# Second layer of a two-layer graph network: row transposes by DMA, block mask and adjacency joined in SBUF

## The chip, the cores and the metric

The kernel runs on one core of one Trainium2 chip. The metric is the device time of one execution in microseconds (us), as the median of the runs taken. Engines have these names in the rows of the profile: PE is TensorE (matmuls) and PEld its weight load, DVE is VectorE, ACT is ScalarE, POOL is GpSimd, SP is the queue that issues most DMAs. Each engine works through its own list of instructions in order; between engines there are semaphores, on which an instruction waits until a count is reached.

## The reference

N = 2048 nodes with D = 256 features; adj is a 0/1 matrix of 2048 x 2048. Both layers are a residual around a normalized input:

```python
h = jnp.maximum(_layernorm(x, axis=-1), 0.0)
x = x + _L0_gnn_ref(h, adj, adj, ...)      # masked attention, plus adj @ (h @ W), gated
h = jnp.maximum(_layernorm(x, axis=-1), 0.0)
x = x + _L1_gnn_ref(h, adj, adj, ptr, Wq, bq, Wk, bk, Wv, bv)
```

The second layer, which the change is about:

```python
mask = graph_id[:, None] == graph_id[None, :]
query, key, value = x @ Wq.T + bq, x @ Wk.T + bk, x @ Wv.T + bv
a = jnp.where(mask, query @ key.T * scale, 0.0)
scores = (a + b + edge_encoding) * jnp.where(mask, 1.0, -1000000.0)
softmax = jax.nn.softmax(scores, axis=-1) * mask
return softmax @ value
```

b and edge_encoding are both adj, and ptr cuts the nodes into 32 graphs of 64, so a row only attends within its graph.

## The kernel before

Every f32 product is made of three f16 products: each operand is split into a high and a low half (xx_high on ScalarE, xx_low on VectorE or GpSimd), and high x high, high x low and low x high are summed in PSUM.

**Stages.** First come the first layer's weights and normalized rows (to about 56 us). Then four column blocks k = 0 to 3 (LAST = 3) of the first layer, with 8 steps q each: attend multiplies the exponents of a pair of row tiles, sums multiplies the adjacency for the next block. ScalarE (raw, high) and VectorE (mask, low) make the exponents of a pair up to four pairs (RING) ahead of TensorE. Behind each block, denominators, keep_a, mix and add_mix form the block's four row tiles of the new x, with their moments; GpSimd takes the inverse deviation (inv_new_deviation, L570) and VectorE the shift (shifts, L1857). keep_b (L1660, L1661) empties a PSUM bank that sums needs again. beside puts small pieces of the second layer between these matmuls.

**The tail.** As a graph lies within a tile of 128 nodes, the second layer needs only the 16 diagonal blocks of 128 x 128, taken as 8 pairs p = 0 to 7 (NQ = 8). For each pair: normalize (L810, ScalarE) writes the f32 rows h1; turn_h1 (L1136) transposes them on TensorE by four f32 transposes into the bank TURN; h1T_high (L816, ScalarE) and h1T_low (L1863, VectorE) split them into f16. keys (L1013) multiplies by the joined query-key weights, keys_high (L823) and keys_low (L1870) split the result. values (L1013, two halves), keep_values (L1882, L1884, with the row constant lift), values_high (L829) and values_low (L593, GpSimd). scores sums, per tile, a mask product of z_same and z_other (L1176), the adjacency by a scaled identity (L1178), and the six f16 products (L1182). maxima (L1891) reduces over the row; row_b is formed from it on VectorE (L1898) or, for p = 1 to 4, on GpSimd (row_bias, L600). exponents (L836, with fo at L841) writes prob; turn_p (L1189) transposes it; pT_high (L846) and pT_low (L1903) split it; gather (L1225) multiplies by the values; row_sums (L611 to L616, GpSimd) gives the sums, and results (L1928, L1933, VectorE) divides by them and adds x. store writes a tile out.

**Order.** It is written out by hand for every engine. In the tail TensorE runs, for p = 3 to 6, turn_h1(p+1), keys(p), values(p, 0), turn_p(p-3), values(p, 1), scores(p-1), gather(p-3). scores(p) waits until pT_low(p-3) has emptied its bank, gather(p) waits for pT_low(p), values_low(p) and for results(p-1). results(p) waits for row_sums(p) first and for gather(p) then. VectorE's list around the start of its loop, and GpSimd's, are these:

```python
            maxima(2)                      # VectorE
            new_moments(LAST, 2, CT)
            for p in range(4, NQ - 1):
                if p > 4:
                    maxima(p - 2)
                results(p - 4)
...
            eng.wait_ge(x1_ready, NT)      # GpSimd
            values_low(2)
            row_sums(0)
            for p in range(4, NQ - 1):
                row_bias(p - 2)
```

## Time and profile before

| | before |
|---|---|
| median of 3 runs | 233.04 us (232.83 to 234.08) |
| profiled execution, first to last instruction | 231.0 us |
| TensorE busy | 222.2 us, 96% |
| VectorE busy | 183.1 us, 79% |
| ScalarE busy | 160.1 us, 69% |
| GpSimd busy | 61.9 us, 27% |
| matmuls, their count | 2042 |

Busy times are sums over one execution. Consecutive instructions of one engine overlap a little at their ends, so the distance between two starts, the pitch, is what an instruction costs its queue. A row of a timeline gives the start, the busy time, engine, line, operation and operands; in square brackets stands how long the engine was idle before it, and what released it. Most buffers of the tail lie in the tensor adjt, so the rows are told apart by their lines.

### The profile page before, as it was taken

The numbers are of one execution on the slowest core, as the hardware profiler recorded it, in microseconds if no ns is written. First come the engines' busy times: TensorE is split into PE (matmuls) and PEld (weight loads), VectorE is DVE, ScalarE is ACT, GpSimd is POOL, SyncE is SP. The second block draws the span as 40 slices with busy tenths as digits, with TensorE's granted clock in tenths as the row PEclk, the third lists the DMA queues.
The fourth block names the chain that finished last, engine by engine and source line by source line (L and its number), as shares of the span: only waits on it lengthen the run. The fifth ranks groups of instructions, "written<-read, shape, count | busy, mean of one in ns | idle before, by whom it ended". The sixth has DMA issues, their size and how long they took to land. (4 is left out here: it accounts for less than half of the span.)

```text
span 231.0 us, 5379 instructions
## 1 busy us (share of the span) xinstructions
PE 222.2 (96%) x2042; PEld 194.5 (84%) x2042; DVE 183.1 (79%) x452; ACT 160.1 (69%) x308; POOL 61.9 (27%) x115
## 2 busy tenths in 40 slices
PE   7899999999999999999999999999999999999971
PEld 6788888888888888888888888888888889999951
DVE  2589778899995967599984499987699949997783
ACT  3768835899966764995651794666995855888760
POOL 4525860000034000001910001730012043576540
PEclk9799999999999999999999999999999999999999
DMA  6999399007989100752400000000000000012123
GB/s 186 359 374 386 113 332 387 15 0 248 285 316 386 44 3 0 259 177 111 173 12 4 0 0 4 1 3 0 3 0 0 3 0 4 0 50 79 48 72 128
DMA packets 20092, 26.34 MB, mean 114 GB/s; under 512 B 1889, under 2 KB 11873, under 8 KB 20065
## 3 DMA queue, kind: packets, MB, share of 16 engines
q1 hardware_dynamic: 19376, 25.71, 32.2%
q8 instruction: 17, 0.28, 0.5%
q10 hardware_dynamic: 688, 0.27, 0.4%
q14 instruction: 11, 0.08, 0.1%
HBM read 23.88 MB, written 2.10 MB: 112 GB/s over the span
## 5 line engine op out<-in xcount | busy, mean ns | idle before, releaser
L1091 PE MATMUL bank_a<-hd,e_hi 128*128 128x257 f16 x256 | 70.3, 274 | 0.0
L1089 PE MATMUL bank_a<-hd,e_hi 128*128 128x257 f16 x256 | 69.7, 272 | 0.0
L1093 PE MATMUL bank_a<-hd,e_lo 128*128 128x257 f16 x256 | 69.4, 271 | 0.0
L1065 PE MATMUL bank_b<-hb,adjt 128*128 128x259 f16 (+1 forms) x512 | 66.5, 273 | 0.2 <-DVE xb L1661 0.2
L1065 PEld LDWEIGHTS bank_b<-hb,adjt 128*128 128x128 bf16 x512 | 49.3, 97 | 7.5 <-DVE xb L1661 0.5
L704 ACT ACTIVATE e_hi<-e_slot 128x1024 f16<-128x1024 f32 x32 | 33.6, 1051 | 26.7 <-PE bank_a L1093 15.6
L1669 DVE SCALAR_TENSOR_TENSOR e_slot<-e_slot,adjt 128x1024 f32<-128x1024 f32 x32 | 39.0, 1219 | 9.0 <-ACT e_slot L697 9.0
L1675 DVE SCALAR_TENSOR_TENSOR e_lo<-e_slot,e_hi 128x1024 f16<-128x1024 f32 x32 | 39.0, 1219 | 7.3 <-ACT e_hi L704 7.2
L697 ACT ACTIVATE e_slot<-s_row,nbias 128x512 f32<-128x512 f32 x64 | 42.3, 709 | 0.2
L570 POOL TENSOR_TENSOR rs_all<-veb,half_neg 128x2 f32<-128x2 f32 x8 | 6.6, 823 | 88.2 <-DVE veb L1848 88.2
L1089 PEld LDWEIGHTS bank_a<-hd,e_hi 128*128 128x128 f16 x256 | 24.7, 96 | 4.0
L1093 PEld LDWEIGHTS bank_a<-hd,e_lo 128*128 128x128 f16 x256 | 25.2, 98 | 3.3
L1091 PEld LDWEIGHTS bank_a<-hd,e_hi 128*128 128x128 f16 x256 | 24.6, 96 | 3.3
L786 ACT ACTIVATE xa<-bank_a,ga 128x256 f32<-128x256 f32 x16 | 6.4, 474 | 10.1 <-DVE ga L1820 10.1
L593 POOL TENSOR_TENSOR adjt<-adjt 128x512 f16<-128x512 f32 x8 | 9.3, 1158 | 14.0 <-ACT adjt L829 14.0
L1013 PE MATMUL bank_b<-w_v,adjt 128*128 128x257 f16 x96 | 12.7, 273 | 0.0
L1013 PE MATMUL bank_a<-wb,x_all 128*128 128x262 f16 x96 | 11.9, 274 | 0.0
L1013 PE MATMUL bank_l<-adjt,w_qk 128*128 128x256 f16 x96 | 11.8, 273 | 0.0
L1013 PE MATMUL bank_a<-wsa,x_all 128*128 128x256 f16 x96 | 11.6, 272 | 0.0
L1870 DVE SCALAR_TENSOR_TENSOR adjt<-bank_l,u_s,adjt 128x256 f16<-128x256 f32 x16 | 7.0, 479 | 5.8 <-ACT adjt L823 5.8
L565 POOL TENSOR_TENSOR ninv<-nsq,half_neg 128x4 f32<-128x4 f32 x1 | 1.9, 1939 | 35.0 <-DVE nsq L1735 35.0
L1013 PEld LDWEIGHTS bank_a<-wb,x_all 128*128 128x128 f16 x96 | 9.2, 98 | 1.5 <-DVE norm_sq L1596 0.2
(238 smaller groups left out, 380.8 us busy)
## 6 DMA issues: line engine op xcount, KB each, us to landing
adjt<-in_adj_t SPq DMA_DIRECT2D x16, 1024.0 KB, 9.1
x_all<-in_x SPq DMA_DIRECT2D x4, 512.0 KB, 5.3
out<-adjt SPq DMA_DIRECT2D x16, 128.0 KB, 1.9
adjt<-in_x SPq DMA_DIRECT2D x3, 512.0 KB, 7.4
diag<-in_adj SPq DMA_DIRECT2D x16, 64.0 KB, 3.6
adjt<-in_x SPq DMA_DIRECT2D x2, 256.0 KB, 3.7
e_slot<-in_L_gnn_W_gcnb ACTq DMA_DIRECT2D x1, 256.0 KB, 4.0
e_slot<-in_W_saT SPq DMA_DIRECT2D x1, 256.0 KB, 4.8
```

The lines of the kernel that those rows point to most:

```text
L570: eng.tensor_tensor(rs_all[:, first:last], veb[:, r0:r1], half_neg[:, 0:r1 - r0], ALU.pow) \
L593: eng.tensor_tensor(v16[:, p % 4, :, 1, :], v32[:, p % 2, :, :], v16[:, p % 4, :, 0, :], ALU.subtract) \
L697: ins = eng.activation(slot_words(g)[:, n * CW:(n + 1) * CW], s_row[:, k * CW:(k + 1) * CW], ACT.Exp, scale=SLOPE - 1.0, bias=nbias[:, j:j ...
L704: eng.activation(high_words(g), slot_words(g), ACT.Copy, scale=E_SCALE).then_inc(hi_ready, 1)
L1013: mm = eng.matmul(bank, left(kk, a), right(kk, b), start=(kk == 0 and a + b == 0), stop=(kk == KT - 1 and a == 1))
L1065: eng.matmul(B[:, r % 2, 0:cols], adjt_block(k, j, r), hb16[:, j, part, 0:cols], start=(j == 0 and part == 0), stop=(j == NT - 1 and part ...
L1089: eng.matmul(A[:, r, 0:D + 1], high, hd16[:, j, 0, 0:D + 1], start=(j == 0), stop=False, skip_group_check=True)
L1091: eng.matmul(A[:, r, 0:D + 1], high, hd16[:, j, 1, 0:D + 1], start=False, stop=False, skip_group_check=True)
L1093: mm = eng.matmul(A[:, r, 0:D + 1], low, hd16[:, j, 0, 0:D + 1], start=False, stop=(j == NT - 1), skip_group_check=True)
L1669: eng.scalar_tensor_tensor(out=slot_words(g), in0=slot_words(g), scalar=1.0, in1=adjt_words(k, 2 * q, 0, PW), op0=ALU.min, op1=ALU.mult) \
L1675: eng.scalar_tensor_tensor(out=low_words(g), in0=slot_words(g), scalar=E_SCALE, in1=high_words(g), op0=ALU.mult, op1=ALU.subtract) \
L1870: eng.scalar_tensor_tensor(out=gT16[:, p % 3, c, 1, :], in0=KEYS[:, c * 2 * P:(c + 1) * 2 * P], scalar=u_s[:, c:c + 1], in1=gT16[:, p % 3, ...
```

## The change

**Transposes.** normalize writes each tile twice on ScalarE, as f32 (h1, now a ring of two pairs) and as f16 (the high half, h1n16), four activations a pair in place of two. h1_low, new on GpSimd, subtracts the two into the low half. SP then issues two transposing DMAs for the pair (turn_h1, SBUF to SBUF), each of 128 partitions x 512 f16, straight into h1T16, which now has room for all 8 pairs. turn_h1 leaves TensorE, h1T_high leaves ScalarE, and h1T_low leaves VectorE. keys and values wait for the DMAs' semaphore. The factor H1_SCALE goes into the inverse deviation. keys alternates between two PSUM banks. The normalize and h1_low calls are placed anew in the lists of ScalarE and GpSimd, and the inverse deviation of the last two tiles stands ahead of row_sums(0).

**Mask and adjacency.** In place of the two matmuls per tile of scores, a tile of k * adjacency minus a huge number outside the graph is made in SBUF in the stage k = 1: spread_gid on TensorE, mark_others and mask_tiles on VectorE, scale_tiles on ScalarE, gid_diag on GpSimd. maxima becomes, per tile, a tensor_tensor_reduce that adds that tile to the scores, writes the sum to prob in SBUF and takes the maximum; exponents works in place there. row_b is formed on VectorE for every pair. turn_onehot and keep_z remain only in the branch for graphs that cross tiles, which this input does not take.

```diff
+        h1T16 = room[:, 2048:6144].bitcast(F16).rearrange("p (a s k n) -> p a s k n", a=NQ, s=2, k=KT)
...
+        def keys_bank(p):
+            return L[:, p % 2, :]
...
+            def turn_h1(p):
+                eng.wait_ge(h1_lo_made, p + 1)
+                for n in range(2):
+                    eng.dma_start_transpose(h1T16_blocks[:, p, :, n * P:(n + 1) * P],
+                                            h1n16_rows[:, p % ROWS, n, :]).then_inc(h1_turned[p % ROWS], 16)
+
+            for p in range(NQ):
+                turn_h1(p)
             for i in range(NT):
...
+            def h1_low(p):
+                eng.wait_ge(h1_ready, 4 * p + 4)
+                eng.tensor_tensor(h1n16[:, p % ROWS, :, 1, :], h1[:, p % 2, :, :], h1n16[:, p % ROWS, :, 0, :],
+                                  ALU.subtract).then_inc(h1_lo_made, 1)
...
-            def row_bias(p):
...
+                if k == LAST:
+                    h1_low(0)
+                    h1_low(1)
+                    h1_low(2)
                 inv_new_deviation(CT * k - CT, CT * k - 2)
+                if k == LAST:
+                    h1_low(3)
                 inv_new_deviation(CT * k - 2, CT * k)
                 if k < LAST:
                     outside(k)
             eng.wait_ge(scale_1_made, SCALES)
+            h1_low(4)
+            h1_low(5)
             values_low(0)
             outside(LAST)
             values_low(1)
             inv_new_deviation(CT * LAST, CT * LAST + 2)
             outer_part(0)
-            row_bias(1)
             outer_part(1)
+            h1_low(NQ - 2)
 
             eng.wait_ge(x1_ready, NT)
             values_low(2)
+            inv_new_deviation(CT * LAST + 2, NT)
             row_sums(0)
             for p in range(4, NQ - 1):
-                row_bias(p - 2)
                 outer_part(p - 2)
                 values_low(p - 1)
                 if p == 4:
-                    inv_new_deviation(CT * LAST + 2, NT)
+                    h1_low(NQ - 1)
                 row_sums(p - 3)
             values_low(NQ - 2)
             outer_part(NQ - 3)
...
-            def normalize(p):
+            def normalize_tile(p, n):
+                i = 2 * p + n
                 eng.wait_ge(nb_ready, 2 * p + 2)
                 if p == 0:
 
                     eng.wait_ge(mask_ready, NQ * LAST)
                     eng.wait_ge(b_summed, CT * LAST)
-                for n in range(2):
-                    i = 2 * p + n
-                    eng.activation(h1[:, p, n, :], x1_all[:, i * D:(i + 1) * D], ACT.Relu,
+                wait(eng, h1_lo_made, p - 1)
+                if p >= ROWS:
+                    eng.wait_ge(h1_turned[p % ROWS], turned(p - ROWS))
+                for into in (h1[:, p % 2, n, :], h1n16[:, p % ROWS, n, 0, :]):
+                    eng.activation(into, x1_all[:, i * D:(i + 1) * D], ACT.Relu,
                                    scale=rs_all[:, i:i + 1], bias=nb_all[:, i:i + 1]).then_inc(h1_ready, 1)
 
-            def h1T_high(p):
-                eng.wait_ge(h1_turned, p + 1)
-                wait(eng, s_summed, p - 3)
-                eng.activation(h1T16[:, p % 4, :, 0, :], TURN.rearrange("p (k n) -> p k n", k=KT), ACT.Copy,
-                               scale=H1_SCALE).then_inc(h1T_hi_made, 1)
+            def normalize(p):
+                normalize_tile(p, 0)
+                normalize_tile(p, 1)
 
             def keys_high(p):
...
-                    wait(eng, p_turned, p - 1)
-                eng.activation(prob[:, p % 2, n * P:(n + 1) * P], score_bank(p)[:, n * P:(n + 1) * P],
-                               ACT.Exp, scale=s_post[:, 0:1], bias=row_b[:, i:i + 1],
+                own = prob[:, p % 2, n * P:(n + 1) * P]
+                eng.activation(own, own, ACT.Exp, scale=s_post[:, 0:1], bias=row_b[:, i:i + 1],
...
+            def scale_tiles(c):
+                if c == 0:
+                    eng.wait_ge(diag_loaded, 16 * NT)
+                    eng.wait_ge(scale_1_made, SCALES)
+                words = diag[:, 8 * c:8 * c + 8, :]
+                eng.activation(words, words, ACT.Copy, scale=k_post[:, 0:1]).then_inc(tiles_made, 1)
...
             keep_a(LAST, 0, 2)
-            h1T_high(2)
             tanh_mix(LAST, 0, 2)
             values_high(1)
             keys_high(2)
             keep_a(LAST, 2, CT)
-            h1T_high(3)
             tanh_mix(LAST, 2, CT)
-            h1T_high(4)
             exponents(0, 0)
             exponents(0, 1)
             keys_high(3)
+            normalize_tile(NQ - 2, 0)
             pT_high(0)
             values_high(2)
             exponents(1, 0)
             exponents(1, 1)
+            normalize_tile(NQ - 2, 1)
             for p in range(4, NQ - 1):
                 values_high(p - 1)
-                h1T_high(p + 1)
                 exponents(p - 2, 0)
                 keys_high(p)
                 pT_high(p - 3)
+                if p == 4:
+                    normalize_tile(NQ - 1, 0)
                 exponents(p - 2, 1)
-                if p in (4, 5):
-                    normalize(p + 2)
+                if p == 4:
+                    normalize_tile(NQ - 1, 1)
             values_high(NQ - 2)
             exponents(NQ - 3, 0)
...
+            def spread_gid(c):
+
+                if c == 0:
+                    eng.wait_ge(norm_1_made, 3)
+                    eng.wait_ge(graphs_made, 6)
+                wait(eng, other_made, c - 1)
+                eng.matmul(L[:, c % 2, :], ones_b[:, :], z_same[:, c * CW:(c + 1) * CW], start=True, stop=True) \
+                   .then_inc(z_summed, 1)
...
-            def turn_h1(p):
-                eng.wait_ge(h1_ready, 2 * p + 2)
...
-                eng.wait_ge(h1T_lo_made, p + 1)
-                wait(eng, g_lo_made, KT * p)
+                eng.wait_ge(h1_turned[p % ROWS], turned(p))
+                wait(eng, g_lo_made, KT * (p - 1))
...
-                    eng.matmul(into, z_same[:, i * P:(i + 1) * P], z_other[:, i * P:(i + 1) * P],
-                               start=True, stop=False, skip_group_check=True)
-                    eng.matmul(into, ident_k[:, :], diag_b[:, bass.ds(2 * i * P + 1, P, 2)],
-                               start=False, stop=False, skip_group_check=True)
                     for kk in range(KT):
                         for a, b in ((0, 0), (0, 1), (1, 0)):
-                            mm = eng.matmul(into, gT16[:, p % 3, kk, a, at:at + P], h1T16[:, p % 4, kk, b, at:at + P],
-                                            start=False, stop=(kk == KT - 1 and a == 1), skip_group_check=True)
+                            mm = eng.matmul(into, gT16[:, p % 3, kk, a, at:at + P],
+                                            h1T16[:, p, b, kk, at:at + P],
+                                            start=(kk == 0 and a + b == 0), stop=(kk == KT - 1 and a == 1),
+                                            skip_group_check=True)
                 mm.then_inc(s_summed, 1)
 
...
+            def mark_others(c):
+                own = slice(CT * c, CT * (c + 1))
+                eng.wait_ge(z_summed, c + 1)
+                eng.tensor_tensor(other[:, own, :], L[:, c % 2, :].rearrange("p (t n) -> p t n", n=P),
+                                  wide(gid[:, own], [P, CT, P]), ALU.not_equal).then_inc(other_made, 1)
+
+            def mask_tiles(c):
+                own = slice(CT * c, CT * (c + 1))
+                eng.wait_ge(other_made, c + 1)
+                eng.wait_ge(tiles_made, c // 2 + 1)
+                eng.scalar_tensor_tensor(out=diag[:, own, :], in0=other[:, own, :], scalar=-MASK_ROOT * MASK_ROOT,
+                                         in1=diag[:, own, :], op0=ALU.mult, op1=ALU.add).then_inc(tiles_masked, 1)
+
             def maxima(p):
                 own = slice(2 * p, 2 * p + 2)
                 eng.wait_ge(s_summed, p + 1)
-                eng.tensor_reduce(neg_mw[:, own], score_bank(p)[:, 0:2 * P].rearrange("p (t n) -> p t n", n=P),
-                                  AX, ALU.max, negate=True).then_inc(mw_ready, 1)
-                if 1 <= p < ROWS_ON_POOL:
-                    return
-                eng.wait_ge(mw_ready, p + 1)
+                wait(eng, p_turned, p - 1)
+                if p == 0:
+                    eng.wait_ge(tiles_masked, NC)
+                for n in range(2):
+                    i = 2 * p + n
+                    eng.tensor_tensor_reduce(out=prob[:, p % 2, n * P:(n + 1) * P],
+                                             in0=score_bank(p)[:, n * P:(n + 1) * P], in1=diag[:, i, :],
+                                             scale=1.0, scalar=-3.0e38, op0=ALU.add, op1=ALU.max,
+                                             accum_out=top_w[:, i:i + 1]).then_inc(mw_ready, 1)
+                eng.wait_ge(mw_ready, 2 * p + 2)
                 eng.wait_ge(lift_ready, p + 1)
-                wait(eng, row_b_ready, p)
-                eng.scalar_tensor_tensor(out=row_b[:, own], in0=neg_mw[:, own], scalar=s_post[:, 0:1],
+                eng.scalar_tensor_tensor(out=row_b[:, own], in0=top_w[:, own], scalar=s_neg[:, 0:1],
...
+                    if k == 1:
+                        if q == 0:
+                            mark_others(0)
+                            mark_others(1)
+                        if q == 4:
+                            mark_others(2)
+                            mark_others(3)
+                        if q in (5, 7):
+                            mask_tiles(q - 5)
+                            mask_tiles(q - 4)
...
             mix(LAST, 2)
             mix(LAST, 3)
             shifts(NT - 4, NT - 2)
-            h1T_low(3)
             maxima(0)
             keep_values(2)
             maxima(1)
-            h1T_low(4)
             add_only(LAST, 2, CT)
             keys_low(3)
             pT_low(0)
                 if p > 4:
                     maxima(p - 2)
                 results(p - 4)
-                h1T_low(p + 1)
+                if p == 4:
+                    shifts(NT - 2, NT)
                 keys_low(p)
                 pT_low(p - 3)
                 keep_values(p)
-                if p == 4:
-                    shifts(NT - 2, NT)
             maxima(NQ - 3)
             results(NQ - 5)
             pT_low(NQ - 4)
             results_last(1)
 
```

## Rows read from the trace of the kernel before

**Rows 1.** The page, part 1: busy us, share of the span, instructions.

```profile
PE 222.2 (96%) x2042; PEld 194.5 (84%) x2042; DVE 183.1 (79%) x452; ACT 160.1 (69%) x308; POOL 61.9 (27%) x115
```

**Rows 2.** Table by stages: stretch, length, busy us of each engine (instructions), clock, DMA.

```profile
190.00:200.00 10.00, 10.00 (x109) 9.17 (x108) 9.16 (x27) 6.82 (x18) 3.52 (x6) 1.00 0.01 2
```

**Rows 3.** Timeline of VectorE, 194 to 228: start, busy us, line, operation, operands.

```profile
194.11 0.88 DVE L1870 SCALAR_TENSOR_TENSOR adjt<-bank_l,u_s,adjt 128x256 f16<-128x256 f32 x2 [0.18 <-ACT adjt L823]
194.90 0.87 DVE L1827 SCALAR_TENSOR_TENSOR xa<-xb,gates,xa 128x256 f32<-128x256 f32 x2
...
196.36 0.41 DVE L1891 TENSOR_REDUCE st<-bank_a 128x2 f32<-128x256 f32 x1
...
202.91 0.15 DVE L1928 RECIPROCAL rz<-st 128x2 f32<-128x2 f32 x1
...
203.89 0.68 DVE L1863 SCALAR_TENSOR_TENSOR adjt<-bank_l,adjt 128x512 f16<-128x512 f32 x1
...
205.32 0.41 DVE L1903 SCALAR_TENSOR_TENSOR adjt<-bank_a,adjt 128x256 f16<-128x256 f32 x1
...
227.21 0.48 DVE L1921 SCALAR_TENSOR_TENSOR adjt<-bank_a,rz,x_all 128x256 f32<-128x256 f32 x1
```

**Rows 4.** Timeline of TensorE, 191 to 218.

```profile
191.71 1.47 PE L1013 MATMUL bank_l<-adjt,w_qk 128*128 128x256 f16 x12
...
205.78 0.83 PE L1225 MATMUL bank_a<-adjt 128*128 128x256 f16 x6
206.45 0.60 PE L1136 MATMUL bank_l<-ident,adjt 128*128 128x128 f32 x4
206.89 1.47 PE L1013 MATMUL bank_l<-adjt,w_qk 128*128 128x256 f16 x12
...
209.74 0.22 PE L1176 MATMUL bank_a<-z_other,z_same 128*128 128x128 bf16 x1
...
209.86 0.49 PE L1182 MATMUL bank_a<-adjt 128*128 128x128 f16 x6
...
215.48 0.82 PE L1225 MATMUL bank_a<-adjt 128*128 128x256 f16 x6
...
217.25 1.47 PE L1013 MATMUL bank_l<-adjt,w_qk 128*128 128x256 f16 x12
```

**Rows 5.** Timeline of VectorE, then of TensorE, around 110 us.

```profile
109.52 0.47 DVE L1661 SCALAR_TENSOR_TENSOR xb<-bank_b,norm_h,bg_row 128x256 f32<-128x256 f32 x1
...
111.64 1.05 PE L1065 MATMUL bank_b<-hb,adjt 128*128 128x259 f16 x8
```

**Rows 6.** Timeline of ScalarE, 198 to 206.

```profile
198.71 0.84 ACT L823 ACTIVATE adjt<-bank_l,u_s 128x256 f16<-128x256 f32 x2
199.44 0.38 ACT L846 ACTIVATE adjt<-bank_a 128x256 f16<-128x256 f32 x1
199.72 0.62 ACT L829 ACTIVATE adjt<-adjt 128x512 f16<-128x512 f32 x1
200.25 0.45 ACT L836 ACTIVATE adjt<-bank_a,st,s_post 128x128 f32<-128x128 f32 x1
...
205.17 1.10 ACT L810 ACTIVATE adjt<-x_all,nb_all,rs_all 128x256 f32<-128x256 f32 x2
```

**Rows 7.** Timeline of GpSimd, 200 to 205.

```profile
200.49 1.16 POOL L593 TENSOR_TENSOR adjt<-adjt 128x512 f16<-128x512 f32 x1 [0.75 <-ACT adjt L829]
201.60 0.20 POOL L611 TENSOR_TENSOR st<-z_off,st 128x2 f32<-128x2 f32 x1
...
202.46 0.71 POOL L600 TENSOR_SCALAR st<-st,s_post,lift 128x1 f32<-128x1 f32 x2
...
204.52 0.72 POOL L570 TENSOR_TENSOR rs_all<-veb,half_neg 128x2 f32<-128x2 f32 x1
```

**Rows 8.** The page, part 6: DMAs, KB each, median us to landing.

```profile
x_all<-in_x SPq DMA_DIRECT2D x4, 512.0 KB, 5.3
out<-adjt SPq DMA_DIRECT2D x16, 128.0 KB, 1.9
```

More of the change, by code:

```diff
@@ L337, in two_graph_layers @@
         z_kept = sem("z_kept")
+        tiles_masked = sem("tiles_masked")
+        other_made = sem("other_made")
         h1_ready = sem("h1_ready")
-        h1_turned = sem("h1_turned")
-        h1T_hi_made = sem("h1T_hi_made")
-        h1T_lo_made = sem("h1T_lo_made")
+        h1_lo_made = sem("h1_lo_made")
+        h1_turned = [sem(f"h1_turned{n}") for n in range(ROWS)]
         v_summed = sem("v_summed")
@@ L413, in low_words, with turned @@
             return e_lo[:, (g % RING) * PW:(g % RING + 1) * PW]
-        TURN, KEYS, VALUES = L[:, 0, :], L[:, 1, :], B[:, :, :]
+        VALUES = B[:, :, :]
         b_norm = L[:, 0, 0:4]
+        def keys_bank(p):
+            return L[:, p % 2, :]
+        def turned(p):
+            return 16 * 2 * (p // ROWS + 1)
+        gid_diag = z_same[:, :].rearrange("p (t n) -> p t n", t=NT)
+        other = z_other[:, :].rearrange("p (t n) -> p t n", t=NT)
         def score_bank(p):
@@ L594, in values_low @@
                    .then_inc(v_lo_made, 1)
-            def row_bias(p):
-                eng.wait_ge(mw_ready, p + 1)
-                eng.wait_ge(lift_ready, p + 1)
-                for c in range(2 * p, 2 * p + 2):
-                    op = eng.tensor_scalar(row_b[:, c:c + 1], neg_mw[:, c:c + 1], s_post[:, 0:1], lift[:, c:c + 1], ALU.mult, ALU.min)
-                op.then_inc(row_b_ready, 1)
             def outer_part(p):
@@ L886, in _ @@
                                        accum_out=sq_1[:, 1:2]).then_inc(sq_1_made, 1)
-                    if k == 0 and q in (4, 6):
-                        keep_z(q - 4)
-                        keep_z(q - 3)
+                    if k == 1 and q in (4, 6):
+                        scale_tiles(q // 2 - 2)
                     if k == 0 and q == 7:
@@ L913, in _ @@
                             keys_high(0)
-                            h1T_high(1)
+                            normalize(5)
                         if q == 6:
-                            normalize(5)
                             values_high(0)
@@ L961, in _ @@
                 eng.wait_ge(o_stored, 16 * NT)
+                for c in range(NC):
+                    keep_z(c)
                 eng.sem_inc(all_v_summed, 1)
@@ L1233, in beside @@
                         norm_1()
[L1234 to L1240 removed]
+                    if q == 6:
+                        spread_gid(place // 2)
+                if k == 1 and q == 3:
+                    spread_gid(2 + place // 2)
                 if k == LAST:
[L1242 to L1243 removed]
                     if q == 5 and place == 2:
@@ L1353, in _ @@
                         attend(k, 1)
-            turn_h1(1)
             values(0, 0)
@@ L1365, in _ @@
             values(1, 1)
-            turn_h1(2)
             for j in range(NT - 4, NT):
@@ L1371, in _ @@
             values(2, 1)
-            turn_h1(3)
             scores(0)
@@ L1375, in _ @@
             for p in range(3, NQ - 1):
-                turn_h1(p + 1)
                 keys(p)
@@ L1399, in _ @@
             with if_general(eng):
+                for c in range(NC):
+                    turn_onehot(c)
+                eng.wait_ge(z_kept, NC)
                 with eng.Fori(0, NT) as i:
@@ L1944, in _ @@
                             mix(k - 1, r)
-                    if k == LAST and q == 3:
-                        h1T_low(0)
                     if g + RING < PAIRS:
@@ L1988, in _ @@
             mix(LAST, 1)
-            h1T_low(2)
             keep_values(1)
```

129 lines of the change are left out of this document (53 added, 76 removed).

## The prediction, made before the changed kernel ran

> **What bounds the kernel now.** I read the page's busy shares first: TensorE is busy 222.2 of 231.0 us [rows 1], Then the table by stages: from 190 to 200 us TensorE is busy all 10.00 us at a granted clock of 1.00, the 2.4 GHz level, VectorE 9.16, ScalarE 6.82 [rows 2]. So TensorE is full and VectorE is nearly full too: time taken off TensorE alone comes back only as far as the other queues can follow. Last the timelines of the five engines in the attention tail, from 180 us, because that is where the change acts. All durations are those of one execution of 231.0 us; the median of the three runs, 233.04 us, lies 2.04 us above it, and I carry those 2.04 us over unchanged. The last result is written from 227.21 us on [rows 3].
>
> **What TensorE loses.** The four f32 transposes of one pair of row tiles, turn_h1, take from 206.45 to 206.89, 0.44 us of TensorE's queue; there are 8 pairs, 3.5 us. The two matmuls per tile for mask and adjacency take from 209.74 to 209.86, 0.12 us; for 16 tiles 1.9 us [rows 4]. Turning the one-hot tiles (16 matmuls of 128 columns) goes, spreading gid (4 of 512 columns) comes: 2048 columns either way, and at 0.06 us per 128 columns (half of those 0.12 us) both are 0.9 us; zero. Of the 5.4 us, all but the last pair's 0.23 us lie ahead of keys(7), so 5.1 us could be gained if TensorE stayed the bound.
>
> **What is added in the masks' stage (k = 1).** Four mark_others and four mask_tiles on VectorE, each a pass over 128x512 like h1T_low's, busy 0.68 us [rows 3] of which the next instruction covers 0.08, so 4.8 us; two scale_tiles on ScalarE over 128x1024, at most four times the 0.38 us of a pass over 128x256 [rows 6]; four keep_z pairs go. The exponents are worked out pairs ahead there, so I cost this at nothing. The nearest deadline is keep_b(2,0): it starts at 109.52, ends at 110.0, and TensorE wants its bank at 111.64 [rows 5]. Two mark_others ahead of it make that 111.2. If that cover were gone it would cost the overshoot, some 0.5 us. gid_diag on GpSimd takes the place of two memsets, where nothing else is due from GpSimd for long.
>
> **What is added in the tail.** normalize writes every tile twice, f32 and f16: one pair before costs 1.10 us for two activations [rows 6], so four cost 2.0 to 2.2 us; I take 0.5 us apiece. The copies h1T_high leave ScalarE, h1T_low leaves VectorE (0.6 us a pair). maxima becomes two tensor_tensor_reduces over 128x128 and, for every pair, row_b. No row shows this instruction. The reduction over 128x256 is busy 0.41 us [rows 3]; half of it, 0.20, is the lower bound, a little over the whole of it, 0.45, the upper, and I take 0.27 us since it handles half the elements. row_bias leaves GpSimd. h1_low comes to GpSimd: a 128x512 subtraction into f16, the same shape as values_low, 1.11 us from 200.49 to 201.60 [rows 7]; 0.9 to 1.3 as bounds.
>
> **The DMA transposes.** SP issues two per pair, each of 128 KB, behind the refills and ahead of all stores; SP waits in turn_h1(p) for h1_low(p), and the stores queue behind. The stores do not matter until the end. The trace has no transposing DMA. A plain 128 KB store lands in 1.9 us, a load of 512 KB in 5.3 us [rows 8]; two transposes lie between 2.4 and 9 us, and I take 4 us. What they may take follows from the queues: pair 2 may take 7.7 us before normalize(4) has to wait for its buffer, pair 3 about 6, pair 6 over 11 and pair 7 about 9 before keys needs them. At 8 us the end moves by 0.8 us, at 9 us by 2.4 and beyond that by about 2 us for each us.
> For the same thing the Trainium skill (VectorE: DVE Perf Modes, The three transpose paths) gives 390 ns on TensorE and 1309 ns by DMA for a 128x128 bf16 transpose. TensorE's in this trace follow each other at 0.11 us, so its figure is no price in a full queue. By its DMA figure, taken one block after the other, the eight blocks of a pair would be 10.5 us, an estimate; by that the kernel would end near 240 us.
>
> **Where it goes wrong: GpSimd's queue.** GpSimd works in order, and the change puts h1_low(6) ahead of values_low(2) and row_sums(0), h1_low(7) ahead of row_sums(1), and moves the inverse deviation of tiles 14 and 15 (0.72 us [rows 7]) ahead of row_sums(0) as well. ScalarE makes normalize(6) between its exponents. I went through the five queues in their order with the pitches of [rows 3, 4, 6, 7] (from one start to the next, which is 0.05 to 0.1 us less than the busy time) and 0.05 to 0.2 us from an end to what waits for it; laid out for the kernel before, the same way puts every keys(p) within 0.2 us of the trace. For the change:
> - keys(2), at 191.71 before [rows 4], starts three turn_h1 earlier, at 190.4, and ends at 191.7. keys_high(2) ends at 192.7; VectorE does keys_low(2) and two mixes (0.8 us the pair of either [rows 3]), the shifts and maxima(0) until 195.3.
> - ScalarE from 195.4 without a gap: exponents(0) 1.0, keys_high(3) 0.73, half of normalize(6) 1.0, pT_high 0.28, values_high 0.53 [rows 6], exponents(1) 1.0, the other half 1.0: done at 200.9.
> - GpSimd: h1_low(6) 1.12, values_low(2) 1.12, inverse deviation 0.70, row_sums(0) 0.87 (201.60 to 202.46 before [rows 7]): done at 204.9 where it was 202.5.
> - VectorE stands at results(0) for it, at 205.0 instead of 202.91 [rows 3], idle some 3.5 us before. Behind it: results 0.98, keys_low(4) 0.79, pT_low(1) 0.33, and so gather(1) on TensorE starts at 207.3, not 205.78 [rows 4], after 4.1 us of standing still.
> - Second turn: the shifts of the last two tiles come behind results(0), at 206.1; half of normalize(7), exponents, the other half end at 208.7; h1_low(7) at 210.0; row_sums(1) at 210.8. results(1) waits for that and gather(2) stands 1.7 us more.
> - No normalize is left, and the queues catch up a little: gather(3) at 217.5 against 215.48, keys(7) at 219.05 against 217.25 [rows 4]. The end, from there on a chain of VectorE and ScalarE as before, is 1.9 us late.
> So the 5.1 us are spent, and 1.9 more: 232.9 us of span and 2.04 around it, 234.9; with the reductions a little over my value 235.0 us.
>
> **Bounds of this case.** The cheap ends together (normalize 0.4 us apiece, h1_low 0.9, reduction 0.20) give +0.4 us, the dear ones (0.55, 1.3, 0.45) +3.8: 233.4 to 236.8 us.
>
> **Rivals.**
> 1. *TensorE stays the bound, faster.* GpSimd's queue would have to be free of the ring above, by h1_low at half of values_low and normalize hidden. For it: TensorE's 10.00 of 10 us [rows 2]. Against: with h1_low at no cost at all the layout still gives only -0.3 us, and with normalize at half its price too -1.7. With the row sums never late it would be -1.1 (VectorE then the bound, see its 9.16 of 10) down to -5.1 if nothing followed late: 228 to 231.9 us. Chance 0.15.
> 2. *The ring closes weakly, no change:* the cheap ends and a mild start give 231.9 to 234.2 us. Chance 0.18.
> 3. *The transposes are slow, slower:* a pair takes over 8 us, normalize(4) and (5) wait for their buffers on ScalarE, and keys_high, values_high and the last denominators queue behind. Decides from 8 us a pair; at 9 us it gives +4.3, 237.3 us, at 10 us +6.3. For it speaks only that no row shows such a DMA; against it that plain transfers of four times the size land in 5.3 us. Chance 0.14.
> 4. *The change does nothing of this:* the tail's code is always run, so no chance of its own.
> The forecast, 234.2 to 237 us, keeps 0.53.
>
> **How the numbers follow.** Forecast 235.0 us. A measurement of this kernel tells about 0.5% (1.2 us) from no change. Faster by over 0.5% is rival 1, 0.15; within it rival 2, 0.18; slower is the forecast and rival 3, 0.67. The range leaves out most of rival 1 and the far end of rival 3: 232.0 to 239.0 us.
>
> **What would show it.** In the changed profile: turn_h1 and both mask matmuls gone from TensorE; TensorE idle some 4 us ahead of gather(1) and 1.7 ahead of gather(2), released by VectorE's pT_low; VectorE idle over 3 us ahead of the reciprocal of results(0), released by GpSimd's row_sums; ScalarE waiting for the last shifts. Wrong it would be if GpSimd's subtraction took well under 1 us, if the reductions took over 0.5 us (then VectorE alone makes it slower still), or if a wait on a transpose stood ahead of normalize or keys.

## The result and the profile after

The changed kernel takes 235.65 us in the median of 4 runs (234.51 to 237.43), the kernel before 232.94 us beside it (232.51 to 234.08): ratio 1.010, 95% interval [1.006, 1.015]. It is slower by about 1%. The profiled execution has a span of 233.6 us in a time of 235.43, so 1.8 us lie around it.

The page of after, part 1 (busy us, share, instructions), answers [rows 1]:

```profile
PE 218.6 (94%) x1966; PEld 189.8 (81%) x1966; DVE 188.7 (81%) x481; ACT 161.7 (69%) x310; POOL 68.1 (29%) x114
```

TensorE has 76 instructions less and is busy 3.6 us less, yet the span is 2.6 us longer: time went into idling. The table by stages of after says where (columns as in [rows 2]; the first three lines were asked for in one view, the last in another):

```profile
20.00:40.00 20.00, 19.15 (x177) 16.50 (x176) 17.44 (x55) 11.81 (x26) 9.64 (x7) 1.00 0.85 303
200.00:210.00 10.00, 6.00 (x51) 4.81 (x49) 5.94 (x22) 6.76 (x20) 5.83 (x9) 0.80 0.14 29
210.00:220.00 10.00, 10.00 (x95) 8.63 (x94) 7.30 (x27) 5.48 (x17) 4.82 (x15) 0.86 0.37 107
```

```profile
206.00:213.00 7.00, 5.56 (x27) 4.10 (x28) 4.42 (x17) 4.48 (x12) 3.86 (x10) 0.51 0.13 27
```

Three things differ from before. In the head, 20 to 40 us, TensorE is busy 19.15 of 20 us, where it had been busy all 20.00. From 200 to 210 us it is busy 6.00 where it had 10.00. And the granted clock, 1.00 in all of these stretches before, is 0.51 in the mean from 206 to 213 us.

The timelines of after in the tail, TensorE, then VectorE, ScalarE and GpSimd (start, busy us, line, operands; in brackets the idle time ahead and who ended it). They answer [rows 3, 4, 6, 7]:

```profile
190.20 1.47 PE L1045 MATMUL bank_l<-adjt,w_qk 128*128 128x256 f16 x12
...
207.44 1.46 PE L1251 MATMUL bank_a<-adjt 128*128 128x256 f16 x6 [4.00 <-DVE adjt L1936]
208.70 2.77 PE L1045 MATMUL bank_l<-adjt,w_qk 128*128 128x256 f16 x12
```

```profile
201.42 0.97 DVE L1869 TENSOR_SCALAR veb<-mvb 128x2 f32<-128x2 f32 x1
...
205.03 0.17 DVE L1961 RECIPROCAL rz<-st 128x2 f32<-128x2 f32 x1 [2.64 <-POOL st L637]
...
230.07 0.48 DVE L1954 SCALAR_TENSOR_TENSOR adjt<-bank_a,rz,x_all 128x256 f32<-128x256 f32 x1
```

```profile
206.30 1.09 ACT L842 ACTIVATE adjt<-x_all,nb_all,rs_all 128x256 f32<-128x256 f32 x2 [3.19 <-DVE nb_all L1879]
```

```profile
201.21 1.16 POOL L616 TENSOR_TENSOR adjt<-adjt 128x512 f16<-128x512 f32 x1 [3.74 <-ACT adjt L842]
202.32 1.16 POOL L621 TENSOR_TENSOR adjt<-adjt 128x512 f16<-128x512 f32 x1
203.44 0.70 POOL L593 TENSOR_TENSOR rs_all<-veb,half_neg 128x2 f32<-128x2 f32 x1
204.10 0.19 POOL L632 TENSOR_TENSOR st<-z_off,st 128x2 f32<-128x2 f32 x1
```

Read them from the bottom. GpSimd makes h1_low(6) (L616), values_low(2) (L621) and the inverse deviation (L593) before it comes to row_sums(0) (L632, done at 205.0). The reciprocal of results(0) on VectorE stood 2.64 us for that, gather(1) on TensorE (L1251) stood 4.00 us for VectorE's pT_low, and ScalarE's normalize(7) stood 3.19 us for the last shifts, which lie behind results(0) on VectorE. keys(5), the line below gather(1), then takes 2.77 us for what takes 1.47 at full clock. The last result is written from 230.07 on, where it was 227.21.

The head, before (TensorE, VectorE, GpSimd) and after (the same):

```profile
33.21 0.27 PE L1306 MATMUL bank_l<-ident,rm 128*1 128x128 f32 x1
34.30 0.38 PE L1309 MATMUL bank_l<-rm,ones 1*128 1x1 f32 x2
```

```profile
32.56 0.17 DVE L1614 COPY s_cols<-hc 128x16 f32<-128x16 f32 x1
```

```profile
30.55 1.80 POOL L563 MEMSET z_other<- 128x2048 bf16 x1
```

```profile
32.58 0.27 PE L1327 MATMUL bank_l<-ident,rm 128*1 128x128 f32 x1
32.68 1.05 PE L1097 MATMUL bank_b<-hb,adjt 128*128 128x259 f16 x8
34.56 0.38 PE L1330 MATMUL bank_l<-rm,ones 1*128 1x1 f32 x2 [0.83 <-DVE rm L1637]
```

```profile
31.62 0.17 DVE L1515 TENSOR_TENSOR hc<-bank_a,col_mul 128x8 f32<-128x8 f32 x1 [0.44 <-ACT hb L705]
31.83 0.18 DVE L1632 TENSOR_REDUCE rm<-hc 128x1 f32<-128x16 f32 x1
31.92 2.30 DVE L1634 COPY s_cols<-hc 128x16 f32<-128x16 f32 x1
```

```profile
30.58 3.61 POOL L584 TENSOR_TENSOR z_same<-ident_b,gid 128x2048 bf16<-128x2048 bf16 x1 [2.36 <-DVE onehot L1523]
```

One copy of 16 columns takes 2.30 us instead of 0.17 and ends at 34.22, 0.03 us after GpSimd's gid_diag (L584, 30.58 + 3.61 = 34.19). TensorE waits 0.83 us for the reduction behind it. Before, the second of GpSimd's two memsets had ended at 32.35, 0.2 us ahead of the same copy.

Executions differ by up to 2.8 us in when their head gets going (the matmul on rm stands at 32.58 us here, at 34.84 in two of those below and at 35.38 in one), and that shifts everything behind. So for profiled executions I also give the *stretch*: from the start of that matmul, bank_l<-ident,rm, to the end of the span. Before it is 231.0 - 33.21 = 197.8 us, after 233.6 - 32.58 = 201.0: 3.2 us longer. It is the stretch of one execution each. How well it repeats can be seen where two kernels do the same: from that matmul to gather(1), after takes 174.86 us and filler (below) 174.87.

### The profile page after: what moved, and what is told of

Read it like the earlier page. It is cut to its first block, busy times and chain, and to the rows that moved or that the text cites. A ratio compares the mean times of both kernels' runs of the same rounds, so it can differ in the third digit from the quotient of the medians.

```text
span 233.6 us, 5279 instructions
## 1 busy us (share of the span) xinstructions
PE 218.6 (94%) x1966; PEld 189.8 (81%) x1966; DVE 188.7 (81%) x481; ACT 161.7 (69%) x310; POOL 68.1 (29%) x114
## 4 chain that ended last, share of the span: by engine, by line
PE 67%; DVE 15%; issue 7%; ACT 6%; POOL 2%; DMA 2%; DVEq 0%; ACTq 0%; POOLq 0%
PE bank_b L1097 21%; PE bank_a L1045 9%; PE bank_a L1123 8%; PE bank_a L1121 8%; PE bank_a L1125 8%; ACT adjt L842 2%; PE bank_l L1045 2%; DVE e_lo L1695 2%; PE bank_l L1037 2%; DVE e_slot L1689 2%; DMA e_slot<-in_gate_w 2%; PE bank_a L1251 2%; DVE xa L1848 1%; PE bank_b L1045 1%; DVE adjt L1886 1%
## 5 line engine op out<-in xcount | busy, mean ns | idle before, releaser
L1125 PEld LDWEIGHTS bank_a<-hd,e_lo 128*128 128x128 f16 x256 | 25.2, 98 | 3.3
L593 POOL TENSOR_TENSOR rs_all<-veb,half_neg 128x2 f32<-128x2 f32 x8 | 7.4, 925 | 67.7 <-DVE veb L1869 67.7
L842 ACT ACTIVATE adjt<-x_all,nb_all,rs_all 128x256 f32<-128x256 f32 (+1 forms) x32 | 16.7, 590 | 3.3 <-DVE nb_all L1879 3.3
L616 POOL TENSOR_TENSOR adjt<-adjt 128x512 f16<-128x512 f32 x8 | 9.3, 1162 | 28.6 <-ACT adjt L842 28.6
L1045 PE MATMUL bank_b<-w_v,adjt 128*128 128x257 f16 x96 | 13.4, 282 | 0.6 <-DVE lift L1900 0.6
L1045 PE MATMUL bank_l<-adjt,w_qk 128*128 128x256 f16 x96 | 13.1, 291 | 0.0
L1045 PEld LDWEIGHTS bank_b<-w_v,adjt 128*128 128x128 f16 x96 | 9.6, 101 | 2.4 <-issue 0.9
```

What stands on the lines that cost most here:

```text
L593: eng.tensor_tensor(rs_all[:, first:last], veb[:, r0:r1], half_neg[:, 0:r1 - r0], ALU.pow) \
L616: eng.tensor_tensor(h1n16[:, p % ROWS, :, 1, :], h1[:, p % 2, :, :], h1n16[:, p % ROWS, :, 0, :], ALU.subtract).then_inc(h1_lo_made, 1)
L842: eng.activation(into, x1_all[:, i * D:(i + 1) * D], ACT.Relu, scale=rs_all[:, i:i + 1], bias=nb_all[:, i:i + 1]).then_inc(h1_ready, 1)
L1045: mm = eng.matmul(bank, left(kk, a), right(kk, b), start=(kk == 0 and a + b == 0), stop=(kk == KT - 1 and a == 1))
L1125: mm = eng.matmul(A[:, r, 0:D + 1], low, hd16[:, j, 0, 0:D + 1], start=False, stop=(j == NT - 1), skip_group_check=True)
```

## The experiments

In every one of them all work is done that the changed kernel does, unless it is said otherwise.

**One part alone.** transposes_only has the DMA transposes with the masks still made by TensorE, mask_only the joined mask with the transposes still on TensorE.

```diff
 # transposes_only, in scores(p): the mask matmuls stay
+eng.matmul(into, z_same[:, i * P:(i + 1) * P], z_other[:, i * P:(i + 1) * P],
+           start=True, stop=False, skip_group_check=True)
+eng.matmul(into, ident_k[:, :], diag_b[:, bass.ds(2 * i * P + 1, P, 2)],
+           start=False, stop=False, skip_group_check=True)
...
 # mask_only, on TensorE: the rows are turned in PSUM, and ScalarE and VectorE copy them
+turn_h1(p + 1)
```

> The transposes' part alone: mask and adjacency stay two matmuls per tile, maxima stays a reduction from PSUM, row_bias stays on GpSimd. Queue theory: the same ring through GpSimd's queue, made longer by row_bias(1) and row_bias(2) ahead of the row sums (0.8 us each): TensorE stands about 5 us ahead of gather(1), its clock falls, and the time is about 4.2 us above the kernel before, 237.1 us: worse than both parts together. Rival, the loss is the reductions' (mask part): no slower than the kernel before, or faster by the transposes' 3.3 us.

> The mask's part alone: the mask and adjacency joined in SBUF, the transposes stay on TensorE with their halves by ScalarE and VectorE. Queue theory: TensorE gives up 1.9 us, but VectorE keeps h1T_low and gets the longer maxima and row_b of every pair, and is full from 190 us on: within 0.3 us of the kernel before, 233.0 us. Rival, TensorE is the only bound: 1.7 us faster, 231.3. Rival, the reductions are the loss: 1 us or more slower.

transposes_only: 236.57 us (235.67 to 238.77), ratio 1.017 [1.012, 1.023], stretch 202.4. mask_only: 233.32 us (231.87 to 235.81), ratio 0.999 [0.995, 1.003], stretch 198.7. TensorE's, ScalarE's and VectorE's timelines of transposes_only, then TensorE's of mask_only:

```profile
207.99 1.46 PE L1265 MATMUL bank_a<-adjt 128*128 128x256 f16 x6 [4.57 <-DVE adjt L1945]
```

```profile
205.40 0.46 ACT L873 ACTIVATE adjt<-bank_a,st,s_post 128x128 f32<-128x128 f32 x1 [4.08 <-POOL st L626]
```

```profile
205.69 1.08 DVE L1892 SCALAR_TENSOR_TENSOR nb_all<-mvb,rs_all 128x2 f32<-128x2 f32 x1
```

```profile
34.66 0.38 PE L1311 MATMUL bank_l<-rm,ones 1*128 1x1 f32 x2 [0.81 <-DVE rm L1622]
```

The slowdown belongs to the transposes' part: alone it is clearly slower than before, while mask_only is level with it. It costs more than both parts together by 0.9 us of the medians and 1.4 us of the stretch, though the two intervals overlap. The stop ahead of gather(1) is 4.57 us, but not as I had expected: row_bias does not make row_sums(0) later (done at 204.66, in the stretch 0.4 us earlier than in after). row_bias(2) behind it (L626) holds ScalarE's exponents(2) until 205.40 and so keys_high(4) until 206.69, and the last shifts, which start beside values_low(3) on GpSimd, take 1.08 us and end at 206.77. VectorE's keys_low(4) needs both; which of the two counts this run doesn't tell. The idle in the head belongs to the masks' part: it is there in mask_only, and transposes_only has none at the same place.

**GpSimd's queue: shorter ahead of row_sums.** low_behind puts h1_low(6) behind row_sums(0) and h1_low(7) behind row_sums(1); low_inv_behind puts the last inverse deviation behind row_sums(0) too.

```diff
 outer_part(1)
-h1_low(NQ - 2)
 eng.wait_ge(x1_ready, NT)
 values_low(2)
-inv_new_deviation(CT * LAST + 2, NT)
 row_sums(0)
+inv_new_deviation(CT * LAST + 2, NT)
+h1_low(NQ - 2)
...
+    row_sums(p - 3)
     if p == 4:
         h1_low(NQ - 1)
-    row_sums(p - 3)
```

(low_inv_behind; in low_behind the line with inv_new_deviation stays where it was.)

> The changed kernel with one reordering on GpSimd: h1_low(6) stands behind row_sums(0) instead of ahead of values_low(2), and h1_low(7) behind row_sums(1). Nothing is added or removed. Queue theory: row_sums(0) is 1.1 us earlier and row_sums(1) no longer waits for the second half of normalize(7); VectorE's wait ahead of results(0) falls from 2.6 to some 1.5 us, TensorE's ahead of gather(1) from 4.0 to 2.3 us, the clock stays at 1.00, and the time falls to about 231.7 us, 1.3 below the kernel before. Rival, VectorE with its new reductions is the bound: no more than 0.5 us gained, 235. Rival, the transposing DMAs hold TensorE up: slower than 235, since both pairs are made later.

> As low_behind, and the inverse deviation of tiles 14 and 15 goes back behind row_sums(0) too. Queue theory: a further 0.7 us off row_sums(0), TensorE's wait ahead of gather(1) about 0.9 us, 230.3 us, 2.7 below the kernel before. Rival, VectorE bound: 235. Rival, DMAs: slower than 235.

low_behind: 232.97 us (230.46 to 235.04), ratio 0.996 [0.992, 1.000], stretch 197.3. low_inv_behind: 232.40 us (229.62 to 232.99), ratio 0.995 [0.991, 0.999], stretch 196.1. TensorE's timeline of low_behind, then of low_inv_behind:

```profile
205.81 0.83 PE L1251 MATMUL bank_a<-adjt 128*128 128x256 f16 x6 [2.19 <-DVE adjt L1936]
```

```profile
207.05 0.83 PE L1251 MATMUL bank_a<-adjt 128*128 128x256 f16 x6 [1.32 <-DVE adjt L1936]
```

The order of two or three calls on GpSimd takes back the whole loss, 2.7 us and more against after; had VectorE with its new reductions or the DMAs been the bound, 0.5 us at most would have come. The stop ahead of gather(1) goes from 4.00 to 2.19 (2.3 expected) and 1.32 us, that ahead of gather(2) is 0.19 and 0.16, and the clock is 1.00 from 200 to 220 us in both. Both fell short in time all the same. For low_behind 231.7 us was expected and 232.97 came; for low_inv_behind 0.9 us of stop and -2.7 us against before were expected, 1.32 and about -1.1 came. 0.8 us of that is the idle in the head, which is in both. Of the rest, a part shows in VectorE's and GpSimd's timelines of low_inv_behind (the third row is VectorE's of low_behind):

```profile
204.84 1.03 DVE L1879 SCALAR_TENSOR_TENSOR nb_all<-mvb,rs_all 128x2 f32<-128x2 f32 x1
```

```profile
204.70 1.15 POOL L616 TENSOR_TENSOR adjt<-adjt 128x512 f16<-128x512 f32 x1
```

```profile
204.49 0.15 DVE L1879 SCALAR_TENSOR_TENSOR nb_all<-mvb,rs_all 128x2 f32<-128x2 f32 x1
```

The last shifts, 128x2, take 1.03 us and end at 205.87, when h1_low(6) has ended (205.85); in low_behind, where h1_low(6) has all but ended when they start (204.58 against 204.49), they take 0.15. It is the picture of the head again: a small VectorE step that starts beside a long GpSimd step ends with it. gid_later, shifts_first and both_clear test it.

**GpSimd's queue: longer.** low_twice makes one more subtraction of h1_low's size ahead of h1_low(6).

```diff
+eng.wait_ge(h1_ready, 4 * (NQ - 2) + 4)
+eng.tensor_tensor(e_slot[:, 0:256].bitcast(F16).rearrange("p (t d) -> p t d", t=2), h1[:, 0, :, :],
+                  h1n16[:, 0, :, 0, :], ALU.subtract)
 h1_low(NQ - 2)
```

> The changed kernel with one more subtraction of h1_low's size (1.15 us) on GpSimd ahead of h1_low(6); its result is used by nothing. Theory (GpSimd's in-order queue sets gather(1)): row_sums(0) and results(0) stand 1.1 us later, TensorE's idle ahead of gather(1) grows from 4.0 to about 5.1 us, time about 1.1 us above the changed kernel: 236.8. Rival (another wait sets gather(1), such as the DMA transposes or the exponents): idle and time do not move, 235.6.

236.38 us (234.67 to 237.96), ratio 1.017 [1.011, 1.022], stretch 201.9, 0.9 longer than after. TensorE's timeline:

```profile
208.61 1.46 PE L1254 MATMUL bank_a<-adjt 128*128 128x256 f16 x6 [5.11 <-DVE adjt L1939]
```

1.11 us more on GpSimd, 1.11 us more of idle ahead of gather(1): this start hangs on GpSimd's queue alone. The medians differ by 0.73 us, under what these runs can part.

**The clock.** filler keeps TensorE busy in the wait.

```diff
+if p == 4:
+    for n in range(64):
+        eng.matmul(L[:, 1, 0:P], ident_b[:, :], ones_b[:, :], start=True, stop=True)
 gather(p - 3)
```

> The changed kernel with 64 bf16 matmuls of 128 columns into an idle PSUM bank ahead of gather(1), that is within TensorE's 4.0 us of idle; their result is used by nothing. Theory (the idle itself brought the granted clock to 0.50 and keys(5) to 2.77 us): the clock stays at 1.00 from 206 to 213, keys(5) takes 1.47, the wait ahead of gather(2) comes back with about 1.5 us, and the time is about 0.9 us below the changed kernel's: 234.8. Rival (the clock's fall costs nothing, because gather(2) would have waited for GpSimd for just as long): 235.6. Third: the matmuls run past the wait and push gather(1): slower, up to 236.5.

235.35 us (233.29 to 237.37), ratio 1.011 [1.006, 1.015], stretch 200.1. TensorE's timeline, and the table by stages:

```profile
204.24 3.74 PE L1401 MATMUL bank_l<-ones_b,ident_b 128*128 128x128 bf16 x64
208.40 0.83 PE L1251 MATMUL bank_a<-adjt 128*128 128x256 f16 x6 [0.43 <-DVE adjt L1939]
209.07 1.47 PE L1045 MATMUL bank_l<-adjt,w_qk 128*128 128x256 f16 x12
...
214.25 0.83 PE L1251 MATMUL bank_a<-adjt 128*128 128x256 f16 x6 [1.49 <-DVE adjt L1939]
```

```profile
206.00:213.00 7.00, 6.33 (x80) 5.61 (x77) 4.63 (x18) 5.20 (x16) 4.04 (x8) 1.00 0.19 39
```

The clock stays at 1.00, gather(1) stands where it stood in the stretch, keys(5) takes 1.47 again, and the wait ahead of gather(2) that I had forecast, and that after doesn't have, is back with 1.49 us. So the fall of the clock filled that wait with slow matmuls and ran over it by 0.9 us of stretch (201.0 against 200.1). By the medians, 0.3 us apart, that 0.9 can't be told from nothing.

**The head.** gid_later lets GpSimd start gid_diag only when VectorE's small copies are done.

```diff
 eng.wait_ge(graphs_made, 5)
+eng.wait_ge(bias_added, 2)
 eng.tensor_tensor(gid_diag, ident_b[:, :].rearrange("p (a n) -> p a n", a=1).broadcast_to([P, NT, P]),
```

> The changed kernel with one wait added: GpSimd starts gid_diag (128x2048, 3.61 us) only after VectorE's two gate biases near 37.7 us, behind its small copies. Theory (VectorE's SBUF-to-SBUF copy L1634 is held off until GpSimd's instruction has ended: it took 2.30 us in the changed kernel, 0.17 before, and ended 34.2, as gid_diag did): L1634 is back at 0.17, TensorE's idle of 0.83 us ahead of L1330 is gone, all later work is 0.7 to 0.9 us earlier, time about 234.8 where the changed kernel has 235.65. Rival (the copy was late for another reason, or the gain is taken by the wait for GpSimd's row sums in the tail, which hangs on the same layout as TensorE): idle ahead of L1330 stays, or the time does not move.

235.26 us (233.98 to 235.62), ratio 1.011 [1.006, 1.015], stretch 199.0. VectorE's timeline, and the table by stages:

```profile
34.19 0.16 DVE L1635 COPY s_cols<-hc 128x16 f32<-128x16 f32 x1
```

```profile
20.00:40.00 20.00, 20.00 (x184) 17.46 (x183) 16.86 (x59) 12.94 (x28) 8.18 (x8) 1.00 0.74 259
```

The copy is back at 0.16 us and TensorE's idle in the head is gone. The stretch is 2.0 us shorter: 1.1 us of it lies ahead of gather(1), and 0.83 of that is the head; most of the rest is the clock, which in this execution fell later and for less long (0.76 in the mean from 206 to 213 us, against 0.51). The stop ahead of gather(1) is 4.00 us as before: head and tail are two matters. The median moved by only 0.4 us and the ratio to before not at all (1.011 against 1.010): that the head's gain reaches the time is not shown by this run.

**The tail's hold-off.** shifts_first is low_inv_behind with h1_low(6) held until the last shifts are made.

```diff
 inv_new_deviation(CT * LAST + 2, NT)
+outer_part(2)
+eng.wait_ge(nb_ready, NT)
 h1_low(NQ - 2)
```

outer_part(2), a small step, also moves ahead of h1_low(6).

> The order that has row_sums(0) and the last inverse deviation ahead of h1_low(6), with h1_low(6) held back once more, until VectorE's last shifts (L1879) are done; outer_part(2) goes ahead of that wait. Theory of the hold-off: in the order without this wait the shifts took 1.03 us for a 128x2 result, beside h1_low(6) on GpSimd (204.70 to 205.85); here they take 0.2, keys_low and pT_low(1) stand 0.8 us earlier, TensorE's wait ahead of gather(1) falls from 1.32 to about 0.5 us, time about 0.7 us below that order's 232.4: 231.7. Rival (only the queue's order counts): L1879 keeps 1 us or the wait ahead of gather(1) stays at 1.3, time 232.4 or, for the later h1_low(6), above.

230.33 us (228.77 to 232.19), ratio 0.989 [0.984, 0.993], stretch 195.5. TensorE's timeline, then VectorE's, then GpSimd's:

```profile
204.17 0.83 PE L1254 MATMUL bank_a<-adjt 128*128 128x256 f16 x6 [0.70 <-DVE adjt L1939]
```

```profile
202.59 0.16 DVE L1882 SCALAR_TENSOR_TENSOR nb_all<-mvb,rs_all 128x2 f32<-128x2 f32 x1
```

```profile
202.83 1.16 POOL L616 TENSOR_TENSOR adjt<-adjt 128x512 f16<-128x512 f32 x1 [0.19 <-DVE nb_all L1882]
```

A wait *added* to GpSimd makes the kernel faster than low_inv_behind: by 0.6 us of the stretch (the expectation was 0.7) and 2.1 us of the medians, which are of different rounds of runs, with intervals that overlap a little. The shifts are back at 0.16 us, and the stop ahead of gather(1) falls from 1.32 to 0.70 us. The rival, that the queue's order alone counts, is out by these two rows. This kernel is the first that is faster than the one before by 1%.

**All together, and the transposes alone in the better order.** both_clear is shifts_first with gid_later's wait; tr_only_ordered is transposes_only with shifts_first's order.

> The order of shifts_first and the later start of gid_diag together, so that no long GpSimd instruction lies beside the VectorE steps it was seen to hold off. Theory: the two effects are in different stages and add: the tail of shifts_first (230.33 us, TensorE's waits 0.70 and 0.17 us ahead of gather(1) and gather(2), clock 1.00) less the 0.83 us of idle in the head: 229.5. Rival: the wait in the head was cover for something else (the loads, the columns' moments), or GpSimd's later start at 37.7 us holds off another VectorE step: 230.3 or above.

> The kernel with the DMA transposes alone (masks by TensorE as before) and the GpSimd order of shifts_first; row_bias(2) and outer_part(2) stand ahead of h1_low(6). Theory (GpSimd's queue and the VectorE hold-off were what made the transposes alone 1.7% slower; what they save TensorE is then worth something): the wait ahead of gather(1) falls from 4.57 to about 2 us, ahead of gather(2) about 1.7, since GpSimd has row_bias too and VectorE's maxima take longer than those of the joined mask; the clock stays at 1.00; time about 233.3, level with the kernel before, 3 us below the transposes alone. Rival (the DMA transposes themselves are late or cost too much): waits released by a transpose, time near 236.6.

both_clear: 229.54 us (228.73 to 232.20), ratio 0.987 [0.980, 0.993], stretch 194.9 (its profiled execution is the longest of the six). tr_only_ordered: 234.17 us (231.48 to 234.92), ratio 1.003 [0.998, 1.007], stretch 198.2. The table by stages of both_clear, then TensorE's, ScalarE's and VectorE's timelines of tr_only_ordered:

```profile
20.00:40.00 20.00, 20.00 (x184) 17.48 (x182) 17.02 (x62) 12.92 (x28) 8.09 (x10) 1.00 0.71 250
```

```profile
207.09 0.83 PE L1269 MATMUL bank_a<-adjt 128*128 128x256 f16 x6 [1.78 <-DVE adjt L1949]
```

```profile
204.51 0.46 ACT L877 ACTIVATE adjt<-bank_a,st,s_post 128x128 f32<-128x128 f32 x1 [1.32 <-POOL st L626]
```

```profile
205.83 0.87 DVE L1903 SCALAR_TENSOR_TENSOR adjt<-bank_l,u_s,adjt 128x256 f16<-128x256 f32 x2 [1.79 <-ACT adjt L864]
```

both_clear beats both kernels, the one before by 1.3% and the changed one by about 6 us of the medians. Whether the head's 0.8 us really add to shifts_first the medians alone leave open (0.8 us apart, intervals overlap); the head's row shows the idle gone, and the stretch is 0.6 us shorter. tr_only_ordered comes back level with before, 2.4 us under transposes_only, with a stop of 1.78 us left. The rows say where it comes from: row_bias(2) on GpSimd (L626) releases ScalarE's exponents(2) only at 204.51, keys_high(4) (L864) stands behind them, and VectorE waits 1.79 us for it. So in the better order it is the two parts together that gain: the masks' part takes row_bias off GpSimd, which is where the transposes' part needs room.

## Why the prediction held, point by point

- *What TensorE loses.* Held: in shifts_first, whose clock is at 1.00 all through the tail, TensorE is busy 216.8 us, the 5.4 laid out less than before. keys(2) starts at 190.20, laid out for 190.4 and at 191.71 before [rows 4]; that the head began 0.63 us earlier here and then stood 0.83 us nearly cancels in it.
- *The masks' stage at nothing.* Held: TensorE is busy 115.97 of 116 us from 60 to 176 us, 116.00 before.
- *normalize, the reductions, h1_low.* Half of normalize is 1.09 us busy for two activations, 0.99 to the next start (0.5 apiece taken). h1_low is 1.16 us busy, 1.11 to the next start (1.12 taken). The reduction was unknown: it is 0.28 us busy and 0.08 for reading its maximum. The second of a pair starts 0.20 us behind the first, and row_b, which waits for both, 0.33 us behind the second: 0.53 us a pair, the 0.27 apiece that I took.
- *The DMA transposes.* Held. A wait on one stands nowhere ahead of normalize or keys. SP's line of after (ns min/median/max of one issue, first and last start) and the time to landing:

```profile
L512 SPq DMA_TRANSPOSE adjt<-adjt x16: 1189/1222/1294, 158.1 to 211.4; - x16
...
DMA to landing us min/median/max: 2.4/2.5/2.5
```

  A pair, issued one behind the other, takes 1.2 + 2.5 = 3.7 us; I took 4. By the Trainium skill's DMA figure (VectorE: DVE Perf Modes, The three transpose paths) I had an estimate of 10.5 us a pair and an end near 240; the rows don't agree when its blocks are taken one after another: four blocks of 128x128 move in one instruction that is 2.5 us on its way. Rival 3 is out.
- *GpSimd's queue*, the step that carried the sum. Held. Laid out: GpSimd starts at 200.9, row_sums(0) done at 204.9, results(0) at 205.0, gather(1) at 207.3 after 4.1 us. Measured: 201.21, 205.0, 205.03, 207.44 after 4.00. low_behind, low_inv_behind and low_twice move this stop by 1.8, 2.7 and 1.1 us and show it as cause. Only the size of VectorE's idle was off (2.64, not 3.5 us).
- *The second turn*, 1.7 us ahead of gather(2): wrong as stated. I had counted every matmul at full clock. After 4.00 us of idle the granted clock is at its 1.2 GHz level, gather(1) takes 1.46 for 0.83 and keys(5) 2.77 for 1.47, and gather(2), at 214.26, has no wait. filler shows the wait where I had it, 1.49 us. The missing term is worth 0.9 us of the stretch (after against filler, one execution each); the medians don't resolve it.
- *gid_diag at zero*, as it takes the place of two memsets and nothing else is due from GpSimd: the step that failed. It looked only at who waits for GpSimd's results, not at who can't work while GpSimd does. In length the two are alike (3.61 us against 1.80 twice), but gid_diag needs the graph numbers and ends at 34.19, where the memsets ended at 32.35, ahead of the copy. VectorE's copy was held for 2.1 us, and TensorE stood 0.83 us. The trace of before had the sign, the other way round: a GpSimd step of 128x4 that takes 0.20 us elsewhere takes 0.93 beside a VectorE pass and ends with it (VectorE's, then GpSimd's timeline):

```profile
109.91 1.22 DVE L1669 SCALAR_TENSOR_TENSOR e_slot<-e_slot,adjt 128x1024 f32<-128x1024 f32 x1
```

```profile
110.26 0.93 POOL L577 TENSOR_TENSOR off_s<-off,inside 128x4 f32<-128x4 f32 x1
```

- *The sum.* Forecast +1.9 us of span. Over the stretch it is +3.2: +1.9, +0.9 for the clock and +0.8 for the head are 3.6. Up to gather(1) the layout holds to 0.1 us: 207.3 - 33.21 + 0.83 = 174.9, measured 174.86. The 0.4 lies behind it: filler, at full clock, takes 25.2 us from gather(1) to the end, where 25.6 were laid out; I did not trace why. In the times this was 235.0 against 235.65 us, and so near it is in part by luck: two terms of 1.7 us together were missing, and the span shows only +2.6 because this execution's head began 0.63 us earlier than that of before.
- *Rival 1*, TensorE stays the bound. Against it I said that h1_low at no cost gives only -0.3; no run makes it free, so that stays untested. But I had looked only at its cost and not at its place: at the same cost, behind row_sums and clear of the shifts, the kernel is 1.1% faster than before (shifts_first), its stretch 2.3 us shorter with the head's 0.8 us of idle still in it. For row sums that are never late I had -1.1.

## What to carry to other kernels

A step that is moved to a lightly loaded engine must be checked against that engine's order, not its load: GpSimd was 29% busy and yet set the end, and four calls in another order with one wait turned 1.0% slower into 1.1% faster. Whenever a long GpSimd instruction is added, look for small VectorE steps beside it whose busy time has grown and which end with it (and the other way round); a wait that keeps the two apart can be a gain. And when a layout shows TensorE idle for some microseconds, price the matmuls behind the gap at the lower clock.

## What the runs showed of the hardware

VectorE and GpSimd shut each other out for some operand forms. VectorE was held until GpSimd's instruction ended in a copy in SBUF (2.30 for 0.17 us), a 128x2 tensor_scalar (L1869 above: 0.97 for 0.17, beside h1_low(6)) and a scalar_tensor_tensor with both inputs in SBUF (1.03 for 0.15). GpSimd was held in L577 above (0.93 for 0.20) until VectorE's pass, with both inputs in SBUF, was over. Not held, in the midst of gid_diag, were L1515, with one input in PSUM (0.17 us), and L1632, a reduction of one input in SBUF (0.18). The Trainium skill (SBUF — State Buffer, Who interferes with whom) states just this: VectorE's copies and tensor_scalar in their two-port modes, and its instructions with two SBUF inputs where the GpSimd instruction reads SBUF, need a port pair that GpSimd shares, and the later one "fully blocks". The rows agree; that it is the port is the page's word, the runs show only who is held and until when. It also speaks against this change in a place where I had priced nothing.

The clock at a stop: TensorE stood 4.00 us ahead of gather(1) both in after and in gid_later. In after the granted clock was 0.50 from about 206.0 us, ahead of gather(1), to 212.9; in gid_later it fell at about 209.2, 0.6 us behind gather(1)'s start, and was back at 212.6. With 2.19 us of idle, in low_behind, it stayed at 1.00. The same stop can thus cost more or less; what decides it these runs don't show.
